# Batch 0's expert products as fp32 products of raw weights, eight raw buffers, and new orders in the last stage

## Time and profile before

| | |
|---|---|
| median of 3 runs | 909.9 us (909.48 to 911.5) |
| profiled execution | 909.54 us |
| its span | 907.8 us |
| mean granted clock of TensorE | 0.986 of full speed |
| busy: PE, PE's weight loads | 866.8 us, 729.4 us |
| busy: ACT, DVE, POOL | 748.7 us, 692.2 us, 639.6 us |
| instructions | 14912 |

### The profile page before, as it was taken

How to read it: one execution, slowest core, us unless ns; L and a number is a source line. 1 busy time by engine, 2 the same in 40 slices (tenths; PEclk the granted TensorE clock), 3 DMA queues, 4 the chain that set the end, 5 groups by cost and what they waited for, 6 DMA issues and landing times.

```text
span 907.8 us, 14912 instructions
## 1 busy us (share of the span) xinstructions
PE 866.8 (95%) x4598; PEld 729.4 (80%) x4598; DVE 692.2 (76%) x1163; ACT 748.7 (82%) x1449; POOL 639.6 (70%) x1031
## 2 busy tenths in 40 slices
PE   6889999999999999999999999999999999877995
PEld 5668888888888888888888888888888888776984
DVE  5777777777777777777777768778898787578675
ACT  3888898888888888888889888988888889665754
POOL 1777767667776777676778866667776677769782
PEclk9999999999999999999999999999999999979898
DMA  6010010101010101001010020000000001332233
GB/s 180 13 43 16 30 31 1 59 1 58 1 59 1 47 13 36 12 19 30 1 30 1 19 58 18 15 18 16 7 24 1 19 1 44 114 82 48 50 37 99
DMA packets 41663, 30.66 MB, mean 34 GB/s; under 512 B 5825, under 2 KB 39649, under 8 KB 41585
## 3 DMA queue, kind: packets, MB, share of 16 engines
q1 hardware_dynamic: 38256, 26.44, 9.7%
q0 software_dynamic: 3328, 3.28, 2.5%
HBM read 20.14 MB, written 9.57 MB: 33 GB/s over the span
## 4 chain that ended last, share of the span: by engine, by line
PE 81%; POOL 6%; DVE 5%; issue 4%; ACT 2%; DMA 1%; POOLq 0%; SPq 0%; DVEq 0%; ACTq 0%
PE t_ps L1580 11%; PE ring_a L1541 6%; PE ring_a L1543 6%; PE ring_a L1542 6%; PE ring_b L1541 6%; PE ring_b L1543 6%; PE u_ps L1541 6%; PE ring_b L1542 6%; PE u_ps L1543 6%; PE u_ps L1542 6%; PE o_ps L1541 2%; PE o_ps L1542 2%; PE o_ps L1543 2%; PE x_ps L1541 2%; PE x_ps L1543 2%
## 5 line engine op out<-in xcount | busy, mean ns | idle before, releaser
L640 POOL TENSOR_TENSOR attn<-prob 128x1024 f32<-128x1024 f32 x128 | 307.4, 2402 | 173.5 <-ACT prob L799 161.8
L1056 DVE TENSOR_TENSOR at_lo<-t_ps,at_hi 128x512 fp32r<-128x512 f32 x253 | 174.1, 688 | 100.7 <-ACT at_hi L782 100.4
L1049 DVE TENSOR_REDUCE negmax<-ring_a 128x1 f32<-128x1024 f32 x128 | 156.7, 1224 | 58.6 <-PE ring_a L1543 55.7
L782 ACT ACTIVATE at_hi<-t_ps 128x512 fp32r<-128x512 f32 x253 | 151.6, 599 | 39.8 <-PE t_ps L1580 38.7
L1049 DVE TENSOR_REDUCE negmax<-ring_b 128x1 f32<-128x1024 f32 x128 | 156.2, 1220 | 2.7 <-PE ring_b L1543 1.1
L1580 PE MATMUL t_ps<-ident,attn 128*128 128x128 f32 x1012 | 152.1, 272 | 4.3 <-DVE at_lo L1056 4.1
L799 ACT ACTIVATE prob<-prob,coef 128x1024 f32<-128x1024 f32 x128 | 147.6, 1153 | 5.7 <-POOL coef L604 5.6
L1580 PEld LDWEIGHTS t_ps<-ident,attn 128*128 128x128 f32 x1012 | 124.4, 140 | 30.0 <-DVE at_lo L1056 9.4
L793 ACT ACTIVATE prob<-ring_a,negmax 128x1024 f32<-128x1024 f32 x128 | 143.1, 1118 | 4.6 <-DVE negmax L1049 4.1
L793 ACT ACTIVATE prob<-ring_b,negmax 128x1024 f32<-128x1024 f32 x128 | 142.4, 1112 | 0.6 <-DVE negmax L1049 0.5
L1541 PE MATMUL ring_b<-xt_hi,q_hi 128*128 128x512 f32 x256 | 112.0, 438 | 0.0
(11 more groups left out here) (450 smaller groups left out, 1792.6 us busy)
## 6 DMA issues: line engine op xcount, KB each, us to landing
attn<-in_L_ffn_w SPq DMA_DIRECT2D x12, 256.0 KB, 3.3
ww_dram<-ww_hi SPq DMA_DIRECT2D x8, 192.0 KB, 2.5
ww_dram<-ww_lo SPq DMA_DIRECT2D x8, 192.0 KB, 2.9
ww_hi<-ww_dram SPq DMA_DIRECT2D x8, 192.0 KB, 2.4
ww_lo<-ww_dram SPq DMA_DIRECT2D x8, 192.0 KB, 2.5
wq_s<-in_L_attn_Wq SPq DMA_DIRECT2D x8, 128.0 KB, 2.7
wk_s<-in_L_attn_Wk SPq DMA_DIRECT2D x8, 128.0 KB, 3.1
xres<-in_L_attn_X SPq DMA_DIRECT2D x2, 512.0 KB, 6.3
```

Source lines behind the costliest of these rows:

```text
L640: pool.tensor_tensor(attn[:, t % AB, :], prob[:, t % 2, 1, :], prob[:, t % 2, 0, :], ALU.add).then_inc(attn_ready, 1)
L782: act.activation(at_hi[:, g % 2, half * GT:(half + 1) * GT, c], t_bank(t, half)[:, :].rearrange("p (k q) -> p k q", q=P), ACT.Copy).then_i ...
L1049: dve.tensor_reduce(negmax[:, par, m:m + 1], ring[m][:, :], axis=AX.X, op=ALU.max, negate=True).then_inc(negmax_ready, 1)
L1056: dve.tensor_tensor(at_lo[:, g % 2, k, c], t_bank(t, half)[:, :].rearrange("p (k q) -> p k q", q=P), at_hi[:, g % 2, k, c].bitcast(F32), A ...
```

## The change

Batch 0's jobs lose the split. `up` and `down` issue one fp32 product of the raw weights with the unsplit rows (`xs_32`, in wq_s and wk_s) and Gelu outputs (`g_32`, in attn) instead of three fp32r products. ACT takes one Gelu, DVE nothing, for those jobs. Batch 1's jobs still use `three`, so the weights are still split.

Each expert's raw weights now have a buffer of their own (raw_a, four in xt_hi and xt_lo, two in at_lo, one in at_hi), loaded right after the last scores (experts 1 to 4) and the last context product (5 to 7). For experts 1 to 7 they are loaded from DRAM copies `w_copy`, which SP makes during batch 0's heads 1 to 7.

In order: `LAST` becomes `[1, 2, 3, 4, 5, 6, 7, 9]`; more of the halves' work is placed among `limit`, `offset`, `tokens`; POOL issues three more batch 0 gathers before its splits and leaves three in them, and only `scatter(0)` stands before batch 1's gathers; SP stores batch 1's rows after all weight loads; 26 products with unused results (`idle_work`) stand among PE's work before the search; at the end DVE does both `add_parts` before y15, ACT all `ln_squares(2, c)` before it copies the sums, and PE's last mixes come later. ACT copies the last rows before it loads the Gelu table.

```diff
-    RAWS = 4
-    LAST = [1, 2, 3, 5, 6, 8, 9, 11]
+    RAWS = 8
+    WSEM = 4
+    LAST = [1, 2, 3, 4, 5, 6, 7, 9]
...
@@ SP @@
+                if k < E:
+                    for w, t in enumerate((w1, w2)):
+                        sp.dma_start(w_copy[w][k], t[k]).then_inc(w_in[0], 16)
...
+                if e == 1:
+                    sp.wait_ge(scores_ready, 2 * TILES)
+                if e == 5:
+                    sp.wait_ge(u_ready, 32)
...
@@ POOL @@
-            for n in range(2, 7):
+            for n in range(2, 8):
                 gather_rows(n // CT, n % CT)
             norm_end(END)
-            for n in range(7, 9):
+            for n in range(8, 11):
                 gather_rows(n // CT, n % CT)
             norm_end(END + GT)
...
-            gather_rows(4, 1)
+            for n in range(11, 13):
+                gather_rows(n // CT, n % CT)
             pool.wait_ge(ln_done, 4)
...
                 if e % 2 == 1:
-                    for k in range(CT):
-                        gather_rows(5 + (e - 3) // 2, k)
-            for q in range(2):
-                scatter(q)
+                    n = 13 + (e - 3) // 2
+                    gather_rows(n // CT, n % CT)
+            scatter(0)
             gather_ready(1)
...
-            for q in range(2, E):
+            for q in range(1, E):
                 scatter(q)
...
@@ ACT @@
+                    if q >= E:
+                        act.activation(up_ps[half], up_ps[half], ACT.Gelu).then_inc(gelu_ready, 1)
...
@@ DVE @@
-            add_parts(0)
-            ln_means(2, 0)
+            for h in range(2):
+                add_parts(h)
+                ln_means(2, h)
             ffn(2 * JOBS + 3)
-            add_parts(1)
-            ln_means(2, 1)
             ln_vars(2, 0)
+            ln_vars(2, 1)
...
@@ PE @@
+                    if q < E:
+                        last_u = pe.matmul(up_ps[half][:, (f % 2) * CAP:(f % 2 + 1) * CAP], raws[q][:, 0, f, :],
+                                           xs_32[q % 2], start=True, stop=True)
+                        continue
...
+                    if q < E:
+                        last_d = pe.matmul(dn_ps, raws[q][:, 1, f, :], g_32[q % 2][:, f, :],
+                                           start=(f == 0), stop=(f == FT - 1))
+                        continue
...
+            def idle_work(dst, count):
+
+                for _ in range(count):
+                    pe.matmul(dst, ww_hi[:, 1, 0:P], ww_hi[:, 1, 0:WWN], start=True, stop=True)
+
+            pe.wait_ge(y_added, 122)
+            idle_work(ring[0][:, 0:WWN], 4)
             x1_transposes(1, 0)
+            idle_work(ring[0][:, 0:WWN], 6)
             rows_in(0)
+            idle_work(ring[0][:, 0:WWN], 2)
             x1_transposes(1, 1)
...
+            down(last - 2)
             limit(1)
+            rows_in((last + 1) // 2 + 1)
+            up(last + 1)
             offset(1)
+            up(last + 2)
             tokens(1)
...
-            ffn(2 * JOBS + 2)
-            mix(JOBS - 2, [0])
-            ffn(2 * JOBS + 3)
-            mix(JOBS - 2, [1])
+            down(2 * JOBS - 3)
+            down(2 * JOBS - 2)
+            mix(JOBS - 3, [0])
+            rows_out(JOBS - 2)
+            down(2 * JOBS - 1)
+            mix(JOBS - 3, [1])
+            rows_out(JOBS - 1)
+            mix(JOBS - 2)
             mix(JOBS - 1)
```

More of the change, by code:

```diff
@@ L195, in build @@
         w_lo = [w_part(q_lo, at_lo, e) for e in range(E)]
-        raws = [a.rearrange("p (w f c) -> p w f c", w=2, f=FT) for a in (raw_a[:, :], *(attn[:, n, :] for n in (0, 2, 3)))]
+        raws = [a.rearrange("p (w f c) -> p w f c", w=2, f=FT)
+                for a in (raw_a[:, :], *(t[:, c * N:(c + 1) * N].bitcast(F32) for t in (xt_hi, xt_lo) for c in range(2)),
+                          *(t[:, 1].rearrange("p k n -> p (k n)")[:, c * N:(c + 1) * N].bitcast(F32)
+                            for t, c in ((at_lo, 0), (at_lo, 1), (at_hi, 1))))]
         g_hi, g_lo = ([t[:, 1].rearrange("p k n -> p (k n)")[:, n * FT * CAP:(n + 1) * FT * CAP].rearrange(
@@ L199, in build @@
         xs_hi, xs_lo = ([xk_part(t, 0)[:, n * CAP:(n + 1) * CAP] for n in range(2)] for t in (xk_hi, xk_lo))
+        xs_32 = [t[:, :, :].rearrange("p m d -> p (m d)") for t in (wq_s, wk_s)]
+        g_32 = [attn[:, 2 + n, :].rearrange("p (f c) -> p f c", c=CAP) for n in range(2)]
         u_hi2, u_lo2 = (xk_part(t, 0)[:, 2 * CAP:2 * CAP + NC] for t in (xk_hi, xk_lo))
@@ L211, in build @@
         tok_row = attn[:, 0, :].bitcast(I32)
-        one_hot = [[xt_hi[:, 0:N], xt_hi[:, N:2 * N]], [xt_lo[:, 0:N], xt_lo[:, N:2 * N]],
-                   *([t[:, 1].rearrange("p k n -> p (k n)")[:, c * N:(c + 1) * N] for c in (2, 3)]
-                     for t in (at_hi, at_lo))]
+        one_hot = [*([t[:, 1].rearrange("p k n -> p (k n)")[:, c * N:(c + 1) * N] for c in (2, 3)]
+                     for t in (at_hi, at_lo)),
+                   [xt_hi[:, 0:N], xt_hi[:, N:2 * N]], [xt_lo[:, 0:N], xt_lo[:, N:2 * N]]]
         tok_f = sb("tok_f", [P, CT, E])
@@ L253, in build @@
         end = sb("end", [P, 1])
+        w_copy = [nc.dram_tensor(f"w_copy{w}", (E, N // 2, P) if w else (E, P, N // 2), F32).ap() for w in range(2)]
         w_dram = nc.dram_tensor("w_dram", (B, E, N), F32).ap()
@@ L321, in build @@
         scattered = [sem(f"scattered{n}") for n in range(2)]
-        w_in = [sem(f"w_in{n}") for n in range(RAWS)]
+        w_in = [sem(f"w_in{n}") for n in range(WSEM)]
         xg_in = [sem(f"xg_in{q}") for q in range(JOBS)]
@@ L850, in xs_round @@
                 need(act, up_ready, 2 * (q - 1))
-                act.activation(xs_hi[q % 2], xs_ps[q % 2], ACT.Copy).then_inc(xs_hi_done, 1)
+                act.activation((xs_32 if q < E else xs_hi)[q % 2], xs_ps[q % 2], ACT.Copy).then_inc(xs_hi_done, 1)
             def y_scale(y):
@@ L856, in y_scale @@
                 if y == 2:
-                    act.wait_ge(w_split, 2 * (RAWS + 1))
+                    act.wait_ge(w_split, 2)
                 if y == 6:
@@ L880, in ffn @@
                     need(act, down_ready, q - 1)
-                    act.activation(g_hi[q % 2][:, f, :], up_ps[half].rearrange("p (f c) -> p f c", c=CAP),
-                                   ACT.Gelu).then_inc(g_hi_done, 1)
-                    act.activation(up_ps[half], up_ps[half], ACT.Gelu).then_inc(gelu_ready, 1)
+                    act.activation((g_32 if q < E else g_hi)[q % 2][:, f, :],
+                                   up_ps[half].rearrange("p (f c) -> p f c", c=CAP), ACT.Gelu).then_inc(g_hi_done, 1)
+                    if q >= E:
+                        act.activation(up_ps[half], up_ps[half], ACT.Gelu).then_inc(gelu_ready, 1)
             for m in range(2):
@@ L969, in _ @@
                 ffn(n)
-            for c in range(GT):
+            for c in range(QT):
                 ln_squares(2, c)
@@ L974, in _ @@
                 act.activation(sum_t[:, h * NC:(h + 1) * NC], mix_ps[h][:, :], ACT.Copy).then_inc(sum_copied, 1)
-            for c in range(GT, QT):
-                ln_squares(2, c)
             for c in range(GT):
@@ L1346, in ffn @@
                     xs_lower(E)
-                if half == 0 and q + 1 < JOBS and q + 1 != E:
+                if half == 0 and E < q + 1 < JOBS:
                     xs_lower(q + 1)
@@ L1926, in _ @@
             counts(1, 1)
-            for n in range(last + 1, 2 * JOBS + 2):
+            rows_out((last + 2) // 2 - 2)
+            down(last - 1)
+            for n in range(last + 3, 2 * JOBS):
                 ffn(n)
```

68 lines of the change are left out of this document (39 added, 29 removed).

## The result

| | before | after |
|---|---|---|
| median of 20 runs each, us | 909.73 (908.74 to 911.76) | 911.48 (909.15 to 915.42) |
| ratio | | 1.0018, 95% interval 1.0011 to 1.0025 |
| profiled execution, us | 909.54 | 911.76 |
| its span, us | 907.8 | 910.0 |
| instructions | 14,912 | 14,785 |

The change makes the kernel 0.18% slower, a little less than the 0.2% set as a bound in the prediction, but the interval of its ratio does not reach 1. The forecast was 909.9, no change. The profiled executions differ by 2.2 us, and the medians by 1.75. The runs of after also scatter more: 6.3 us between the fastest and the slowest, against 3.0.

What follows compares the result with a forecast made beforehand. It took POOL's gathers and scatters, released by DVE's batch 1 search, as the bound, with PE ending within 1 us. Terms -2.4+1.05+1.95-0.2 = +0.4 on 909.54 gave 909.9 us, range 906.8 to 912.9.

Steps and rivals of the forecast that it cites:

- POOL's term: Batch 1's gathers start at 835.8, 14 scatters follow; last scatter starts at 883.5 instead of 885.92: -2.4 us.
- the smaller orders: At the end, a variance moved ahead and ACT's earlier squares free POOL's last powers: -0.2 us.
- the clock's term: PE idles 4.9 us before y15's mixing, which then runs at half clock, 3.9 us instead of 1.95: +1.95 us.
- The front: Before the search: moved gathers delay the second LN power 1.15 us, but full clock brings first count at 808.2, -0.2.
- at nothing: Parts counted as costing no time: weight copies, raw weight loads, 26 idle products where PE waits, one_hot's new order.
- The search: DVE's batch 1 threshold search: 2.41 us a level, eighth vote at 828.2 instead of 833.63, index at 835.8.
- The cheap product: Rival: the 256-column fp32 product costs 0.22 us, PE never presses, POOL bounds; 909.5 us, chance 0.05.
- PE: Batch 1's first transposes at 844.2 instead of 849.38; y14's mixing ends at 888.7, leaving PE idle 4.9 us.
- The end: Both residual adds on DVE before y15 put its scaling at 892.5 and its mixing at 893.6: +1.05 us.
- the clock falls in the search: Rival: half clock on PE between votes makes two levels late, index 3.2 us later; 913.1 us, chance 0.13.
- POOL slips: Rival: moved gathers cost the front 2 to 3 us, or their rows land late; 911.2 us, chance 0.1.
- all goes right: Rival: the front doesn't slip, POOL is 1.0 us earlier and the clock holds; 907.0 us, chance 0.07.

Runs made afterwards that it cites:

- f1: The changed kernel run once more with no edit; 911.97 us, 1.0017 of the kernel before.
- e4: The changed kernel without the six idle products between the first expert products and the gate rows' transposes; 910.79 us, 1.0012 of the kernel before.
- e3: The changed kernel with job 1's two scatters put back ahead of batch 1's gathers on POOL; 909.62 us, 0.9993 of the kernel before.
- f3: The changed kernel without six idle products behind the first expert products, with three behind each half of the gate's products instead; 912.32 us, 1.0021 of before.
- f2: The changed kernel with satisfied waits added as pads on SP (64) and DVE (4 per batch 1 half); 910.23 us, 1.0003 of before.
- e1: The changed kernel with only the last part's orders on DVE and ACT as before; 910.72 us, 1.0008 of the kernel before.
- f4: Changed kernel with job 1's scatters before batch 1's gathers, one half before last vote, no six idle products, earlier last-part orders, SP/DVE pads; 906.9 us, 0.9962.
- e2: The changed kernel with twelve idle products between PE's mixing of y14 and y15; 911.49 us, 1.0019 of the kernel before.
- e7: The changed kernel without any of its 26 idle products, on the slower second chip; 918.32 us, 0.9968 of the kernel before.
- e6: Changed kernel with job 1's scatters before batch 1's gathers, one half before last vote, no six idle products, earlier last-part orders; second chip, 918.88 us, 0.9971.
- e8: The changed kernel with 64 satisfied waits on SP ahead of the accumulator's loads, on the slower second chip; 920.68 us, 0.9985 of before.

## Why the prediction was wrong

The forecast was the same as before, with the sum -2.4+1.05+1.95-0.2 = +0.4. Measured: -0.94+1.05+1.40-0.1, and +0.8 that was not in it. Of the 1.8 us between the two sums, POOL's term has 1.5, the one that was missing 0.8 and the smaller orders 0.1; the clock's term gives 0.55 back. Two terms carry the miss: POOL's, and the one that was missing.

- **The front.** Measured +1.1 on the powers, as far as the front's 0.5 earlier start is counted (forecast 1.15). First count forecast 808.2, came at 809.21. **This step failed:** I took the clock as 1.00 from the idle products on and let the row transposes follow the rows at once. It is 1.00 up to 802.6 only. From DVE's gate step to the first count I had 4.15 us; it took 5.67 in after, and 4.05 in f1, where the clock held. Six of the idle products I had put "at nothing, where PE waits anyway" did stand on the path in after, 1.05 by e4, but only because of the half clock: in f1 PE waits there, as I had said.
- **The search.** A level of 2.40 (forecast 2.41), the fp32 product of 256 columns 0.43 as taken (823.21 to 824.08 is 0.87 for two), and only the last vote late. The four passes of "FP8 and Floating Point Precision" (TensorE Precision Notes) in the Trainium skill, 0.43 by my estimate, agree with it. The cheap product is out. From vote to gather 8.27 (8.0), and the 0.4 that the first half of the indices was to save didn't come: the gather starts 0.03 behind the second half, although the code waits for the first only. Why is open, but the kernel before does the same (second half done at 842.12, gather at 842.15), so its rows could have told.
- **POOL. This is the step that decided.** The term of -2.4 measured -0.94. "Index and POOL arrive nearly together": the index came at 837.5, not 835.8 (1.0 from the first count, 0.7 behind the last vote), and POOL was free at 833.8, not 835.4. The gathers start at the later of the two, so the index's 1.7 us are the miss of this term. By my sum the move of scatter 1 was free of charge, since with it ahead POOL would have come to the gathers only at 839.3; in fact it had 3.7 us of idle there for its 3.9 us of work. Gathers and scatters themselves took 22.51 and 1.92 each (22.25, 1.96). e3 puts it back, and its median falls by 1.86 us.
- **PE.** It came at 892.7, not 888.7. The late votes are 1.05 of that and the half clock from 836.7 on some 1.6 (in e4 and f3, where it didn't fall there, y14's mixing ends 1.7 earlier beyond what the first count gives); most of the rest is the wait of 1.41 for ACT ahead of it. So the gap was 2.38 and not 4.9, and the clock fell all the same in this execution: 1.40 for 1.95. I had named a late PE as what would save the clock. So the fall came as forecast, but by luck: f1 and f2 (2.60 and 2.45, no fall) say that a gap of 2.4 to 2.6 can go either way. In e1, e3 and f4 (1.49, 0.52, 0.41) it didn't fall.
- **The end.** +1.05 measured 1.05. -0.1 for -0.2 up to the normalized rows; another 0.2 came behind them, hidden under the next term.
- **What no term had:** the code fetches in the last transfer, 1.05 us, 0.8 with the 0.2 of the orders. The trace of before has none there and so couldn't point to them; the changed count of instructions by engine could have.

Of the rivals, "the clock falls in the search" happened: not in the profiled execution, but in those of e2, f1 and f2, at 1.0 to 1.2 us a fall and at one level, not two (e7, without idle products, lost 0.3 there). "POOL slips" did not; "all goes right" stays the measure of what the change had to give, and f4 got past it (907.0 forecast, 906.9) with another order and the fetches gone.

## What to carry to other kernels

When a change speeds up one of two chains that meet, work out the arrival of the other from its own rows, and look for work that the new wait could cover before anything is moved behind it; here 3.7 us of POOL stood idle beside 3.9 us of work moved away. A gain ahead of the bound lengthens a gap behind it, and the clock can then take it back, as in f3. Where a profile of one execution shows a fall of the clock, profile a second execution before you put the fall down to an edit, and compare instruction counts by engine when the tail of the program has changed.

## What was not expected of the hardware

- The clock fell to 0.50 where PE had just been busy for 5.2 of 5.5 us (797 to 802.5 in after), behind the gate's products of eight columns, and stayed there to 806.0 although PE worked on. With six idle products of 384 columns among them it held (f3); it also held once without (f1).
- Two fetches of 8 KB of instructions, one within an output transfer of 1 MB and one behind it, go with an end that is 1.05 us later; behind the transfer a thin stream of some 20 GB/s goes on. Satisfied waits added ahead of it removed both (f2).
- A chip on which the same program takes 11.6 us more. The four traces there show waits and half clock from 850 to 869 and, in e6, to beyond 872, and nothing of it before. There is no trace of the kernel before on it, so the place is shown for the variants alone.
- The pace of POOL's chain from first gather to last scatter was 47.5 us in after and 48.3 where it began earlier (e4, f3), but 48.4 in e8, which began later on the second chip; what slows it is open.
